# A graph layer's kernel on one core: the edge targets loaded ahead of the tiles' statistics, the last tile's blocks in another order, and its last store on another queue

## The reference

```python
h = jnp.maximum(_layernorm(x, axis=-1), 0.0)
xn = _batchnorm(h, norm1_g, norm1_b)
agg = segment_sum(xn[src], dst, num_segments=N) / max(deg, 1)
conv_out = relu(agg @ W_conv + b_conv)
# linear attention over 256 nodes, 8 heads of 64, 256 random features
q, k, v = heads(h, Wq), heads(h, Wk), heads(h, Wv)
attn = phi(q) @ (phi(k)^T v) / (phi(q) . sum phi(k))   # then @ Wo
out = x + _batchnorm(conv_out + h_attn + h, norm2_g, norm2_b)
```

## Time and profile before

| | us |
|---|---|
| three runs, median | 176.44 (176.09 to 176.51) |
| the profiled execution, its own time | 176.07 |
| its span | 174.2 |
| TensorE busy (matmuls) | 165.6 (95%) |
| VectorE, ScalarE, GpSimd busy | 137.9, 89.9, 7.6 |
| mean granted TensorE clock | 0.996 |

### The profile page before, as it was taken

The page is one execution under the profiler, slowest core; times in us unless marked ns, Lnnn a source line. Parts: engine busy times, 40 slices in busy tenths (PEclk is TensorE's granted clock), DMA queues, the critical chain, the costliest instruction groups (busy, mean ns, idle before and its releaser), DMA issues.

```text
span 174.2 us, 3024 instructions
## 1 busy us (share of the span) xinstructions
PE 165.6 (95%) x1131; PEld 108.9 (63%) x1132; DVE 137.9 (79%) x315; ACT 89.9 (52%) x163; POOL 7.6 (4%) x22
## 2 busy tenths in 40 slices
PE   7899999999999999999999999999999999999960
PEld 2388877545545546557777798684464574767940
DVE  2868889989947786999656785975999998597981
ACT  3426999839694779979416164217600505004050
POOL 5037000000000000000000000000000000000000
PEclk9999999999999999999999999999999999999998
DMA  5997970000610000000000000000294014050046
GB/s 186 362 328 185 346 261 0 0 4 0 218 43 0 4 0 0 0 4 2 0 4 0 0 4 0 0 4 4 70 336 186 0 28 119 6 147 0 4 124 172
DMA packets 11884, 13.71 MB, mean 79 GB/s; under 512 B 1458, under 2 KB 6748, under 8 KB 11868
## 3 DMA queue, kind: packets, MB, share of 16 engines
q1 hardware_dynamic: 10476, 12.13, 21.3%
q10 hardware_dynamic: 1072, 1.10, 1.8%
q0 software_dynamic: 320, 0.26, 0.7%
HBM read 10.92 MB, written 2.56 MB: 77 GB/s over the span
## 4 chain that ended last, share of the span: by engine, by line
PE 88%; DVE 3%; ACT 3%; DMA 2%; issue 1%; DVEq 0%; ACTq 0%
PE bank L978 24%; PE bank L708 20%; PE bank L638 8%; PE bank L659 4%; PE bank L732 4%; PE bank L722 4%; PE bank L751 4%; PE bank L685 4%; PE bank L650 3%; PE bank L630 3%; PE bank L1005 2%; PE bank L696 2%; DMA xs<-in_x 2%; DVE gl L1222 1%; DVE st L1054 1%
## 5 line engine op out<-in xcount | busy, mean ns | idle before, releaser
L978 PE MATMUL bank<-r,gh 128*128 128x512 f16 (+8 forms) x140 | 39.3, 314 | 0.0
L978 PE MATMUL bank<-r,gl 128*128 128x512 f16 (+8 forms) x140 | 39.3, 313 | 0.0
L708 PE MATMUL bank<-wc,xs 128*128 128x512 f32 (+1 forms) x80 | 38.5, 608 | 0.2 <-DVE gl L1222 0.2
L1085 DVE TENSOR_TENSOR ohb<-iota,bcol 128x1280 f16<-128x1280 f16 x25 | 20.5, 818 | 3.7 <-PE bank L650 3.7
L708 PEld LDWEIGHTS bank<-wc,xs 128*128 128x128 f32 (+1 forms) x80 | 13.6, 187 | 11.6 <-issue 11.6
L392 ACT ACTIVATE r<-bank 128x500 f16<-128x500 f32 x25 | 18.3, 764 | 3.4 <-PE bank L650 3.4
L978 PEld LDWEIGHTS bank<-r,gh 128*128 128x128 f16 (+1 forms) x140 | 13.5, 97 | 8.5 <-issue 0.3
L978 PEld LDWEIGHTS bank<-r,gl 128*128 128x128 f16 (+1 forms) x140 | 13.6, 97 | 8.2
L608 ACT ACTIVATE bw<-mv,epst 128x1 f32<-128x1 f32 x4 | 1.2, 295 | 31.0 <-DVE mv L1385 31.0
L638 PE MATMUL bank<-hT,r 128*128 128x256 f32 x64 | 14.5, 381 | 0.0
L650 PEld LDWEIGHTS bank<-ohv,ohb 128*128 128x128 f16 x250 | 9.7, 98 | 6.7 <-issue 5.3
(11 more groups left out here) (177 smaller groups left out, 267.1 us busy)
## 6 DMA issues: line engine op xcount, KB each, us to landing
xs<-in_x SPq DMA_DIRECT2D x15, 256.0 KB, 4.6
out<-xs SPq DMA_DIRECT2D x7, 256.0 KB
r<-in_L_gnn_Wq SPq DMA_DIRECT2D x1, 1024.0 KB, 7.5
r<-in_L_gnn_Wk SPq DMA_DIRECT2D x1, 1024.0 KB, 5.7
wc<-in_L_gnn_W_conv SPq DMA_DIRECT2D x1, 1024.0 KB, 9.1
wvo<-in_L_gnn_Wv SPq DMA_DIRECT2D x1, 1024.0 KB, 11.2
wvo<-in_L_gnn_Wo SPq DMA_DIRECT2D x1, 1024.0 KB, 5.3
xs<-in_x ACTq DMA_DIRECT2D x3, 256.0 KB, 4.2
```

The costliest lines, as they stand in the source:

```text
L708: last = nc.tensor.matmul(acc[0:n, :], xnT[:, f, i * P:i * P + n], wc[:, f, :], start=(f == 0), stop=(f == FT - 1))
L978: last = nc.tensor.matmul(acc[:, 0:cn], gg[0:n, s, f * P:(f + 1) * P], A16[0:n, s, c0:c0 + cn], start=(s == 0 and gg is gh), stop=(s == NT ...
L1085: last = V.tensor_tensor(oh[:, s0:s0 + n, :].rearrange("p s (m t) -> p s m t", t=2), iota16[:, 0:size].rearrange("p (m t) -> p m t", t=2). ...
```

## The change

Five edits, in the order of the stages.

- **Loads.** The targets move from second place on SyncE's queue to first place on ScalarE's; tile 1 moves from first place on ScalarE's to second place on SyncE's. Wk waits for tile 7 in place of tile 9.
- **Edge search in two halves.** VectorE waits for the targets first of all, makes the thresholds in three parts (3, 2 and 5 of the 10), the first ahead of the statistics of tiles 0 and 1, the second ahead of their scales, the third after them. TensorE does the first half of the search ahead of tile 0's transposes, and the second half after tile 1's; the two partial counts are added on VectorE, which is one small instruction more. TensorE's constant products become 15, and 1 after the first half, in place of 18 and 3.
- **Tile 1 on VectorE.** VectorE scales tile 1 (without the ReLU), and applies the ReLU while it stores the turned tile into hT.
- **Last tile's blocks.** TensorE turns (2,2), (2,0), (2,1) in place of (2,1), (2,2), (2,0). VectorE scales nodes 0 to 511 of the last tile, ScalarE 512 to 767, 768 to 1023 and the rest.
- **Last store.** SyncE's queue stores all of block (3,2), its last 98 rows too.

```diff
-ROUSE, ROUSE_MORE = 18, 3
+SEARCHED = 5
+ROUSE, ROUSE_LATE = 15, 1
...
-        first = sb("first", [P, 2], F32)
+        first = sb("first", [P, 4], F32)
...
-        order = [("hT", 0), ("hT", 1), ("first",), ("q", 0), ("q", 1), ("hT", 2), ("hT", 3), ("hT", 4), ("hT", 5),
+        order = [("first",), ("hT", 0), ("hT", 1), ("q", 0), ("q", 1), ("hT", 2), ("hT", 3), ("hT", 4), ("hT", 5),
...
-        order_end += [("agg", FT - 1, c) for c in range(len(LAST_CHUNKS))] + [("zT", FT - 2, j) for j in (1, 2, 0)]
+        order_end += [("agg", FT - 1, c) for c in range(len(LAST_CHUNKS))] + [("zT", FT - 2, j) for j in (2, 0, 1)]
...
+        n1_ready = sem("n1_ready")
...
-            sp.dma_start(edst[:, :], dst.rearrange("(p j) -> p j", p=EP)).then_inc(dst_in, 16)
+            load_x(1)
...
-            sp.wait_ge(x_in[NT - 1], 16)
+            sp.wait_ge(x_in[7], 16)
...
-                        for i in range(8, NT if f < FT - 1 else 9):
+                        for i in range(8, NT):
...
-            for i in (1, 3, 5):
+            act.dma_start(edst[:, :], dst.rearrange("(p j) -> p j", p=EP)).then_inc(dst_in, 16)
+            for i in (3, 5):
...
-            ln_tile(1)
...
-            store_hT(1)
...
-                for a, b in ((0, 512), (512, 1024), (1024, N)) if f < FT - 1 else ((0, 256), (256, 512), (1024, N)):
+                for a, b in ((0, 512), (512, 1024), (1024, N)) if f < FT - 1 else ((512, 768), (768, 1024), (1024, N)):
...
-            stored(act, "zT", FT - 1, 2)
-            act.dma_start(out[(NT - 1) * P:N, c], xs[0:LAST, NT - 1, c]).then_inc(o_out, 16)
...
-                pe.wait_ge(h_ready, i + 1)
+                if i == 1:
+                    pe.wait_ge(n1_ready, 1)
+                else:
+                    pe.wait_ge(h_ready, max(i, 1))
...
-            def edge_search():
-                pe.wait_ge(nb_ready, 1)
-                acc = pe_open(pe, "first")
+            def edge_search(half):
+                pe.wait_ge(nb_ready, half + 2)
+                if half == 0:
+                    pe_open(pe, "first")
+                acc = bank[uses[("first",)][0]]
+                a, b = ((0, SEARCHED), (SEARCHED, EJ // GR))[half]
...
-                    for j in range(EJ // GR):
-                        last = nc.tensor.matmul(acc[0:GROWS, hf:hf + 1], below[:, j, hf * GROWS:(hf + 1) * GROWS],
-                                                cone[0:EP, 0:1], start=(j == 0), stop=(j == EJ // GR - 1))
-                last.then_inc(full("first"), 1)
+                    for j in range(a, b):
+                        last = nc.tensor.matmul(acc[0:GROWS, 2 * half + hf:2 * half + hf + 1],
+                                                below[:, j, hf * GROWS:(hf + 1) * GROWS], cone[0:EP, 0:1],
+                                                start=(j == a), stop=(j == b - 1))
+                if half:
+                    last.then_inc(full("first"), 1)
...
+            edge_search(0)
+            rouse(ROUSE_LATE)
...
-            edge_search()
-            rouse(ROUSE_MORE)
+            edge_search(1)
...
-                    elif j == 1:
+                    elif j == 0:
...
-                        if f == FT - 1 and i in (0, 2):
-                            pe.wait_ge(z_act, 3 * f + i // 2 + 1)
+                        if f == FT - 1 and i in (4, 6):
+                            pe.wait_ge(z_act, 3 * f + i // 2 - 1)
...
-            transpose_z(FT - 2, (1, 2))
+            transpose_z(FT - 2, (2,))
...
+            transpose_z(FT - 2, (1,))
...
+            def normal_second():
+                dve.wait_ge(ln_ready, 1)
+                V.tensor_scalar(xs[:, 1, :], xs[:, 1, :], lnw[:, 2, 1:2], lnw[:, 3, 1:2], ALU.mult, ALU.add).then_inc(n1_ready, 1)
+
+            def store_second():
+                acc = landed(dve, "hT", 1)
+                V.tensor_scalar(hT[:, :, P:2 * P], acc[:, :].rearrange("p (t n) -> p t n", t=FT), 0.0, None, ALU.max
+                                ).then_inc(read("hT", 1), 1)
+
...
-                V.tensor_scalar(first[0:GROWS, :], acc[0:GROWS, 0:2], -1.0, 0.0, ALU.add, ALU.max).then_inc(read("first"), 1)
+                V.tensor_copy(first[0:GROWS, :], acc[0:GROWS, 0:4]).then_inc(read("first"), 1)
...
-                V.tensor_scalar(rows[0:GROWS, :], first[0:GROWS, :], float(ROW_MAX), None, ALU.min).then_inc(rows_ready, 1)
+                link(V.scalar_tensor_tensor(out=first[0:GROWS, 0:2], in0=first[0:GROWS, 0:2], scalar=-1.0, in1=first[0:GROWS, 2:4],
+                                            op0=ALU.add, op1=ALU.add))
+                V.tensor_scalar(rows[0:GROWS, :], first[0:GROWS, 0:2], 0.0, float(ROW_MAX), ALU.max, ALU.min).then_inc(rows_ready, 1)
...
-            def edge_thresholds():
-                dve.wait_ge(dst_in, 16)
-                link(V.tensor_copy(edst2[:, :, :], edst[:, ::GR].unsqueeze(2).to_broadcast([EP, EJ // GR, 2])))
-                shape = [EP, EJ // GR, NW // 2, 2]
-                V.tensor_tensor(below[:, :, :].rearrange("p j (w t) -> p j w t", t=2),
-                                edst2[:, :, :].unsqueeze(2).to_broadcast(shape),
+            def edge_thresholds(a, b):
+                shape = [EP, b - a, NW // 2, 2]
+                V.tensor_tensor(below[:, a:b, :].rearrange("p j (w t) -> p j w t", t=2),
+                                edst2[:, a:b, :].unsqueeze(2).to_broadcast(shape),
...
+            dve.wait_ge(dst_in, 16)
+            link(V.tensor_copy(edst2[:, :, :], edst[:, ::GR].unsqueeze(2).to_broadcast([EP, EJ // GR, 2])))
+            edge_thresholds(0, 3)
...
+            edge_thresholds(3, SEARCHED)
...
-            edge_thresholds()
+            normal_second()
+            edge_thresholds(SEARCHED, EJ // GR)
+            store_second()
...
-                V.tensor_scalar(yT[:, f, 512:1024], yT[:, f, 512:1024], s2[:, f:f + 1], t2[:, f:f + 1],
+                V.tensor_scalar(yT[:, f, 0:512], yT[:, f, 0:512], s2[:, f:f + 1], t2[:, f:f + 1],
```

## The result

The changed kernel took 176.83 us (median of 20 runs, 176.10 to 179.36), the kernel before 176.16 beside it (20 runs). The ratio is 1.0044, with an interval of 1.0029 to 1.0060: slower by 0.8 us (0.67 by the medians alone), where 0.9 us faster was forecast.

A forecast was written before the change was run, and what follows sets the result against it. TensorE bounds 88% of the span, leaving gains only in the first 11 us and last 8. Head -0.30 and tail -0.58 sum to -0.88 us: 175.2 on the profiled execution's scale, median 175.55, range 174.8 to 176.3.

The forecast's parts named there:

- the head's -0.30: Head: queries start at about 10.54 instead of 10.83, with the list landing at 4.1; gain 0.3 us.
- the tail's -0.58: Tail: 0.33 us from earlier additions and 0.25 from the last store's queue; from 0.3 to 0.7 together.
- rival 5: Clock falls while TensorE idles before tile 0's transposes; queries at 1.2 GHz cost 2.4 us, giving 177.95; chance 0.02.
- the argument against rival 5: Ahead of the last tile TensorE idled 1.26 us with the clock granted at 1.00 (0.23 busy of 1.5 us).
- the rule against an early list: Head: the list cannot land clearly ahead of tile 0's share on its engines; head gains at most 0.35 us.
- Rival 2: List at 4.3 to 4.7 or tile 1 past 5.4: head about nil, tail kept, 175.9 us; chance 0.20.
- The 0.3 survives: After the head: slack covers extra VectorE work, so the 0.3 us gain reaches the long TensorE-bound middle.
- Wk was costed at nothing: Head: Wk, issued two tiles sooner, lands earlier than the keys ask; worth nothing, could only hurt the gathers.
- Rival 4: Gathers fall behind Wk, Wc and Wv, 2.5 us later; costs about 0.8 of the gain, 176.4 us; chance 0.05.
- The earlier addition: Tail: last tile's first block reaches VectorE at 168.48 for 168.81, 0.33 us earlier, carried through three additions.
- its bytes move right behind those of tile 2: Tail: store (3,0), issued 0.33 us earlier, follows tile 2's bytes directly; from there the stream carries the same 640 KB.
- The last store's queue: Tail: last 49 KB issued on SyncE instead of ScalarE join the stream; gain 0.25 us, low end 0, high 0.36.

The follow-up runs named there:

- a2: Changed kernel with five constant products in place of one after the first half search, filling the pause ahead of tile 0's transposes; 176.32 us, ratio 0.9994.
- a1: The changed kernel run again, unaltered, against the kernel before; 177.08 us, ratio 1.0046.
- a4: Changed kernel with the tail of the kernel before, so H alone; 176.65 us, ratio 1.0043 to the kernel before.
- b3: Changed kernel with 18 constant products at the start in place of 15, still one after the first half search; 176.71 us, ratio 1.0024.
- e2: c1 with only block (3,2) stored of output block columns 2 and 3; 175.23 us, ratio 0.9943 to the kernel before.
- H: Everything in the change except T, including Wk after tile 7; measured alone as a4, 176.65 us, ratio 1.0043.
- T: The change's tail edits: block order, scaling of the last tile, last store; measured alone as a3, 176.42 us, ratio 0.9995.
- a3: Kernel before with T alone, its head unchanged; 176.42 us, ratio 0.9995.
- b4: Kernel before with 12 constant products at the start in place of 18, its three later ones kept; 178.73 us, ratio 1.0127.
- b1: Changed kernel with 8 constant products at the start and none after the first half search, in place of 15 and 1; 179.46 us, ratio 1.0153.
- d2: c1 with output block column 2 not stored; 175.66 us, ratio 0.9965 to the kernel before.
- c1: Kernel before with T and with Wk waiting for tile 7; 176.04 us, ratio 0.9982.
- b2: Kernel before with one edit, Wk waiting for tile 7 in place of tile 9; 176.15 us, ratio 0.9984.
- d1: Kernel before with output block column 2 not stored; 176.31 us, ratio 1.0015.
- e1: b2 with only block (3,2) stored of output block columns 2 and 3; 175.38 us, ratio 0.9953 to the kernel before.
- e3: b2 with output block column 2 not stored; 176.36 us, ratio 1.0002 to the kernel before.
- f1: c2 run once more, unaltered, against the kernel before; 176.31 us, ratio 1.0008.
- f2: c2 with 20 constant products at the start in place of 18; 175.95 us, ratio 0.9987 to the kernel before.
- c2: c1 without the three constant products ahead of the queries; 175.84 us, ratio 0.9976 to the kernel before.

## Why the prediction was wrong

The forecast of -0.88 was the head's -0.30 and the tail's -0.58. Neither arrived: with the pause filled, the changed kernel takes what the kernel before takes (a2, 0.9994). The clock, which the forecast left out, adds the rest (0.7 to 0.8 us).

**The side was decided by rival 5, which had a chance of 0.02.** "The clock falls while TensorE idles some 1.2 us before tile 0's transposes, and queries run at 1.2 GHz" is in the main what happens, by the spans and clocks in 8 of 20, 4 of 12 and 3 of 12 executions (after, a1, a4), at a price of 1.70 us in b3's profile in place of 2.4. One detail differs: in b3 and e2 the fall comes behind the pause, not in it. b3's pause ends at 9.31 and the clock falls at about 11.7, e2's ends at 8.15 and it falls at about 10.8. Shown: the loss goes with H and not with T (a3, a4); filling the pause leaves no long execution in twelve, with all else of the change in (a2); three more at the start do not (b3); a pause made in the kernel before brings it there (b4); and four profiles hold the fall itself (b1, b3, b4, e2; those of after, a1 and a4 are all of quick executions).

The mean clock of a single execution tells less than it seems to. In every profile the clock goes to half once more at the end, after TensorE's last product, and that alone gives means of 0.988 (a2) to 0.997 (a3); e2 has 0.988 with a fall in the head. It is the two groups that tell: the 15 long executions of after, a1 and a4 have 0.969 to 0.988, the 11 long ones of the kernel before 0.988 to 0.996.

**The step that failed** is the argument against rival 5: the earlier trace rows show the clock at 1.00 over 1.5 us with little work ahead of the last tile. One execution in which the clock held told nothing of how often it holds. Nor does dense work ahead of a pause keep it: behind the last product the clock falls within 0.6 us in a2, 1.05 us in after and 3.3 us in the profile of before, whose fall stands in the earlier trace rows as 0.81 (a pause of 1.1 to 1.3 us ahead of the last tile, and that tile's turning, stand just before).

The Trainium skill, "TensorE: Matmul & The Clock Gate", "Part 1: The HAM clock gate", says that the window over which the chip judges TensorE's activity runs freely, so that the moment of a transition varies from run to run, and puts this at half a microsecond either way. The traces agree on the variation and show more of it: the weight loads of the constant products come 0.43 us apart at first and 0.21 apart later, and the first close one was at 4.07 (e2), 4.91 (d2), 5.45 (before) and 7.14 (c1), 3.1 us apart. When the pace doubles early, a fixed number of products is used up sooner and TensorE idles longer behind it: 0.26 to 0.29 us ahead of the first half search and 0.97 ahead of the transposes in a4 and b3 (doubled at 4.94 and 4.95), none and 0.75 in after (not doubled before 6.7). That may be a part of why one program has two kinds of executions, but it is not shown, and it does not suffice: a4 has the same pauses as b3, and no fall. What decides stays open. In b3 and e2 the loads had landed late as well (the list's cast at 4.76, tile 0's statistics at 4.28, each the latest of its head).

**The head, -0.30 forecast, nil at the full clock.** Two things were off. The list landed for casts that start at 4.29, 4.19, 4.07, 4.67, 4.76 and 4.49 (after, a1, a4, a2, b3, b1): median 4.4, for 4.1. In each of these the cast starts 0.3 to 0.5 us after the landing of tile 0, never ahead of it, as the rule against an early list in the prediction would have it; no run separates that rule from other causes. And the base was one execution. Tile 0's statistics start at 4.07 in the earlier trace rows, but at 3.78 to 3.84 in six of the ten other profiles with 18 products ahead of it (4.28 at the latest), and its queries at 10.54 to 10.76 in those of b2, a3, c1, d1, d2, e1 and e3, which leave the head as it was apart from Wk, for 10.83 in the earlier trace rows (e2, where the clock fell, has 11.29). The changed head's queries at the full clock, 10.73, 10.63 and 10.51 in after, a1 and a4 and 11.11 in a2, are no earlier. The steps from the list to the queries held: cast to statistics 0.65 forecast and 0.68 measured, statistics to transposes 3.90 and 3.86, transposes to queries 1.89 and 1.90. Rival 2's head, nil, is what came at the full clock.

**"The 0.3 survives" failed too.** The cover was looked for at tile 9, the columns and 35.11, but not at the bank that the keys need: in after they start as soon as VectorE's read of it is done. That the added VectorE work made this read late is not shown, since the head of before has it start anywhere from 18.76 to 19.54 and waits for it in e1 and e3 as well (0.41 and 0.34 us). f1 and f2 show the same limit from the other side: queries 0.4 to 0.6 us earlier than in b2 and c1 gave keys at most 0.2 earlier, with a wait for that bank in front. Wk was costed at nothing, and cost nothing; the profiles of a3 and d1 (0.92 and 0.98 us) show that its old condition sometimes delays the keys. That the 24 spans of b2 and c1 stop at 174.9 fits, where 11 of 128 of the kernel before lie at 175.5 or more, but the intervals of both include 1. Rival 4 was wrong: in after the gathers landed in 6.9 to 7.3 us.

**The tail, -0.58 forecast.** Times from VectorE's last small operation ahead of the last tile (t, 166.86 in the profile of before), one profile each:

| stores in the tail | old tail: last addition, end | new tail: last addition, end |
|---|---|---|
| all | 3.57, 7.31; a4 7.05, b2 7.13, b4 7.42 | 3.23, 7.07; a1 7.10, a2 7.14, a3 7.18, b1 7.05, b3 7.16, c1 7.58, c2 7.03, f1 7.07, f2 7.15 |
| without block column 2 | 7.55 (d1), 7.61 (e3) | 6.93 (d2) |
| only (3,2) | 6.09 (e1) | 5.93 (e2) |

The earlier addition is right to 0.01 (0.34 for 0.33). The end is not: with all stores the means are 7.23 and 7.15, so 0.1 us arrives, less than the profiles scatter. Without block column 2 the new tail ends 0.6 earlier than the old. With the last block alone stored (e1) the end comes 1.1 earlier after the same additions, and the new tail gains 0.16 (e2). The windows of d2, where nothing but the last tile is stored:

```profile
170.00:171.00 1.00, 0.00 (x0) 0.00 (x0) 0.48 (x2) 0.00 (x0) 0.00 (x0) 1.00 0.41 112
171.00:172.00 1.00, 0.00 (x0) 0.00 (x0) 0.00 (x0) 0.00 (x0) 0.00 (x0) 1.00 1.01 294
172.00:173.00 1.00, 0.00 (x0) 0.00 (x0) 0.00 (x0) 0.00 (x0) 0.00 (x0) 0.52 0.87 236
```

Its first store is issued at 169.64, bytes move about 1 us later, and the last tile's own 625 KB fill all 16 engines until about 172.9. With block column 2 stored as well, four windows of before and of after tell the two tails apart, at 3.3 and 5.7 us behind t (before), 2.1 and 5.7 (after):

```profile
170.16:170.46 0.30, 0.00 (x0) 0.00 (x0) 0.28 (x1) 0.00 (x0) 0.00 (x0) 1.00 0.12 31
172.56:172.86 0.30, 0.00 (x0) 0.00 (x0) 0.00 (x0) 0.00 (x0) 0.00 (x0) 0.83 0.63 166
...
169.22:169.52 0.30, 0.27 (x2) 0.03 (x1) 0.30 (x2) 0.00 (x0) 0.00 (x0) 1.00 0.17 46
172.82:173.12 0.30, 0.00 (x0) 0.00 (x0) 0.00 (x0) 0.00 (x0) 0.00 (x0) 0.50 0.08 22
```

The old tail is not held up by tile 2: its stores have drained (share 0.12) before the bytes of the last tile move, 3.6 us behind t, and in d1 and e3, where tile 2 is not stored, they begin at the same 3.6. That is why leaving 625 KB out gains nothing there; why d1 and e3 even end 0.2 to 0.3 later than the profile of before stays open. In the new tail the gap lies 1.2 us earlier, and from there the engines stay full until about 5.6 us behind t (c1 has a share of 0.93, 1.08 and 0.95 from 169 to 172). So the step that failed is "its bytes move right behind those of tile 2", with the whole 0.33 carried to the end. The bulk of the bytes does end earlier (share 0.08 for 0.63 in the same window behind t), but a thin remainder moves on for 0.6 us, at shares of 0.08 and 0.04 (in before for 0.3 us, at 0.07), and the span's end comes only 0.1 earlier on average. What stretches the remainder was not tried.

**The last store's queue, 0.25 forecast, measured nothing.** From last addition to end: e1 (both queues) 2.52, e2 (SyncE alone) 2.70, one profile each. With all stores SyncE issues the two in 0.82 us mostly, but in 1.46 (b3), 1.45 (f2) and 1.70 (c1) at times, as ScalarE had issued one in 1.01 to 1.68. That is the low end that the prediction named, "slow because of the stream, not of the engine"; c1, with its 1.70, ends latest. The Trainium skill, "DMA: Bandwidth & Descriptors", "Issuing engines are not separate DMA queues", says that the DMAs of all issuing engines run on the same 16 DMA engines, so that another issuer saves issue time alone. e1 and e2 agree: the move brought no earlier end.

The prediction also counts the last tile's stores as 640 KB; its own terms, 256+256+64+49, make 625. Nothing hangs on it.

## What to carry to other kernels

Where warm-up products (the constant products that nobody reads) cover a wait, a change upstream of that wait changes the pause behind them. Before counting the gain, count the idle time that the new order leaves on TensorE, in the latest landing and with the products at their fastest pace. Take the base of a head that begins with loads from several executions, or give its terms the spread of a landing: here 0.5 us for tile 0, more than the 0.3 that the head was to gain. And look at the spans and clocks of all runs, since one profile of a kernel with two kinds of executions shows one kind.

## What the runs showed of the hardware

- Over the first constant products the granted clock reads 1.00 in the windows of all nineteen profiles, while they come 0.43 us apart, and 0.21 later: the ratio of the two levels, 1.2 and 2.4 GHz. At the start the column does not show the pace; the spacing of the weight loads does.
- At the end, in all nineteen profiles, the granted clock goes to half 0.6 us (a2) to 3.8 us (a3) after TensorE's last product, behind 150 us of nearly full use and the pause ahead of the last tile (1.13 us in after).
- The granted clock, once down at half, stayed there for 3.4 us in b3 and e2, 6.8 in b4 and 10.2 in b1, by their windows.
- Removing 625 KB of stores from the old tail left its time where it was (e3, 1.0002), and removing another 512 KB took off 1.0 us (e1 175.38, e3 176.36).
- The list of 78 KB in 125 rows, at the head of its queue, was there for its cast 3.3 to 4.0 us after its issue, no sooner than a 256 KB tile lands (3.3 and 3.5 in the earlier trace rows, 3.0 to 3.6 beside it).
